# A list of its own in DRAM for the halves of x, a first gather from it, and the last routing ahead of the last two chunks' masks

## The reference

```
qkv = xn @ w_attn.T                      # heads of 16 numbers, 16 heads
phi(x) = elu(x) + 1
per chunk of 128 tokens:
    scores = phi(q) phi(k)^T, masked to the causal half
    num = scores v + phi(q) S ;  den = scores.sum + phi(q) z ;  S += phi(k)^T v ;  z += phi(k).sum
y = (num / den) @ w_proj.T
top  = argmax(xn @ gate_w.T + gate_b + expert_bias)
ffn  = relu(xn @ w1[top] + b1[top]) @ w2[top] + b2[top]
out  = x + y + ffn
```

## Time and profile before

| what | value |
|---|---|
| median of the runs | 510.94 us (509.48 to 511.06) |
| the profiled execution's own time | 512.02 us |
| its span, first to last instruction | 510.2 us |
| what lies around the span | 1.8 us |
| PE, DVE, ACT, POOL busy | 95, 76, 55, 60 % of the span |
| first `g1` of slot 0 | 287.25 us |

### The profile page before, as it was taken

How to read it: one execution, slowest core, us unless ns; L and a number is a source line. 1 busy time by engine, 2 the same in 40 slices (tenths; PEclk the granted TensorE clock), 3 DMA queues, 4 the chain that set the end, 5 groups by cost and what they waited for, 6 DMA issues and landing times.

```text
span 510.2 us, 17893 instructions
## 1 busy us (share of the span) xinstructions
PE 486.4 (95%) x6293; PEld 403.4 (79%) x6293; DVE 389.6 (76%) x849; ACT 280.7 (55%) x540; POOL 307.3 (60%) x497
## 2 busy tenths in 40 slices
PE   7699999999999999999998699999999999999996
PEld 6578887788878888788877678888888888888884
DVE  3678898988989888898789177766776776776774
ACT  3447887888887878877885033333333333333330
POOL 5666888889898798878763523344344344344222
PEclk9989999999999999999999899999999999999999
DMA  8614575665665665655443512132212212210000
GB/s 260 221 44 120 182 212 168 194 190 180 201 176 169 191 195 186 200 168 183 135 148 106 188 35 75 53 90 68 66 56 65 84 53 79 74 50 28 22 17 2
DMA packets 34306, 62.91 MB, mean 123 GB/s; under 512 B 5677, under 2 KB 10030, under 8 KB 34096
## 3 DMA queue, kind: packets, MB, share of 16 engines
q1 hardware_dynamic: 29232, 49.17, 30.9%
q0 software_dynamic: 4992, 12.60, 8.2%
HBM read 51.00 MB, written 13.50 MB: 126 GB/s over the span
## 4 chain that ended last, share of the span: by engine, by line
PE 88%; DVE 3%; issue 3%; POOL 2%; ACT 2%; DMA 1%; DVEq 0%; POOLq 0%; ACTq 0%
PE ps L654 21%; PE ps L667 20%; PE ps L401 8%; PE ps L516 6%; PE ps L443 6%; PE ps L472 6%; PE ps L456 5%; PE ps L419 4%; PE ps L486 4%; PE ps L502 3%; PE ps L623 2%; PE ps L426 1%; PE ps L508 1%; PE ps L384 1%; DMA AR<-scr,AR 1%
## 5 line engine op out<-in xcount | busy, mean ns | idle before, releaser
L654 PEld LDWEIGHTS ps<-AR,W 128*128 x1872 | 131.5, 99 | 40.2 <-issue 1.2
L654 PE MATMUL ps<-AR,W 128*128 128x128 f16 x1872 | 155.9, 220 | 0.9 <-ACT AR L1216 0.9
L667 PE MATMUL ps<-W,ST 128*128 x624 | 150.5, 326 | 0.7 <-DVE ST L1057 0.7
L1225 ACT ACTIVATE ST<-ST 128x512 f16<-128x512 f32 x78 | 49.2, 630 | 104.6 <-DVE ST L1045 103.0
L1386 POOL DMA_INDIRECT out<-AR x39 | 39.8, 1021 | 106.4 <-DVE AR L1077 105.2
L1045 DVE SCALAR_TENSOR_TENSOR ST<-ps,TAs,B1S 128x512 f32<-128x512 f32 x78 | 58.4, 749 | 52.1 <-PE ps L654 49.6
L753 DVE TENSOR_TENSOR AR<-ps,CT 128x512 f32<-128x512 f32 x128 | 82.0, 684 | 3.2 <-PE ps L443 3.2
L1321 POOL TENSOR_TENSOR W<-ST,W 128x512 f16<-128x512 f32 x64 | 74.8, 1169 | 12.5 <-ACT W L1159 6.3
L1381 POOL DMA_INDIRECT AR<-scr,AR x39 | 50.1, 1285 | 31.4 <-issue 12.8
L1057 DVE SCALAR_TENSOR_TENSOR ST<-ST 128x512 f16<-128x512 f32 x78 | 53.6, 687 | 15.6 <-ACT ST L1225 15.6
L401 PE MATMUL ps<-xT,WA 128*128 128x128 f16 x768 | 48.9, 221 | 3.4 <-ACT xT L1109 3.4
(11 more groups left out here) (147 smaller groups left out, 787.0 us busy)
## 6 DMA issues: line engine op xcount, KB each, us to landing
ST<-in_w SPq DMA_DIRECT2D x128, 256.0 KB, 4.2
scr<-XR SPq DMA_DIRECT2D x32, 256.0 KB, 2.1
XR<-in_x SPq DMA_DIRECT2D x32, 128.0 KB, 4.6
AR<-in_b SPq DMA_DIRECT2D x1, 1024.0 KB, 5.3
AR<-in_wall SPq DMA_DIRECT2D x2, 388.0 KB, 4.1
AR<-scr,AR POOLq DMA_INDIRECT x39, 3.6
out<-AR POOLq DMA_INDIRECT x39
ST<-in_cst SPq DMA_DIRECT2D x1, 576.0 KB, 4.8
```

The costliest lines, as they stand in the source:

```text
L654: a = e.matmul(dst, W[:, off:off + 57472][:, bass.ds(place_of(s), 128)], XT16[s % 2][:, xl * 256 + k * 128:xl * 256 + (k + 1) * 128], star ...
L667: a = e.matmul(PS[4 + s % 2][:, 0:w], src[h % 4][:, fs], W[:, off:off + 57344 + w][:, bass.ds(place_of(s), w)], start=(f == 0 and w == 512 ...
L1225: e.activation(HH[h % 4], H32[h % 2], ACT.Relu).then_inc(a_hh, 1)
```

## The change: what it does

The two halves of x get a DRAM list of their own, `scr16`, which SP fills chunk by chunk once they are made (32 more stores of 128 KB). The first NX0 = 3 slots take the halves from it, by gathers of their own (`gather_x16`) into `X0`, so that they need no result of the attention; the whole rows are still gathered from `scr` for every slot, into NG = 8 buffers now (they are the `XR` buffers), for `rest` in slots 0 to 2 and for everything from slot 3 on. DVE routes group 3 in the last turn and right behind it, ahead of the masks of chunks 30 and 31. PE moves `place(3)` and the 32 matmuls for `ids` up, and the last two steps of chunk 31's attention (`yt2`, `pr`) between the pieces of slot 0. ACT and POOL take the last eight quarters behind the loop, in a new order. `rest(s)` moves one slot later.

```diff
+        NG, NX0 = 8, 3
+        XG = [XR[(5 + i) % 8][:, :] for i in range(NG)]
+        X0 = [XR[4][:, 0:256].bitcast(F16)] + [WAF[:, 512 * i:512 * i + 512] for i in range(NX0 - 1)]
 # SP
+            def store_x16(c):
+                e.wait_ge(S["xl"], c + 1)
+                e.dma_start(scr16[c * 128:(c + 1) * 128, :], X16[c % R]).then_inc(d_s16[c % R], 16)
...
+            store_res(NC - 3)
+
+            e.wait_ge(S["pv"], NC)
             e.dma_start(B2, b2).then_inc(d_b2, 16)
+            store_res(NC - 2)
+            store_res(NC - 1)
 # PE, behind the loop
+            place(3)
+            inter(NC - 2)
+            warm(70)
+            (the 32 matmuls for ids)
             yt1(NC - 3)
-            inter(NC - 2)
-            yt2(NC - 3)
             pv(NC - 2)
             scores(NC - 1)
+            yt2(NC - 3)
             pr(NC - 3)
...
             yt1(NC - 1)
-            warm(24)
-            yt2(NC - 1)
-            pr(NC - 1)
 # PE, second phase
+                if s < NX0:
+                    e.wait_ge(d_g16[s], 16)
+                    x16 = X0[s]
...
+                if t == 3:
+                    yt2(NC - 1)
+                if t == 5:
+                    pr(NC - 1)
 # DVE, second phase
+                if s == 0:
+                    res(NC - 1)
...
-                    rest(s)
+                if 1 <= s <= NS:
+                    rest(s - 1)
 # ACT, behind the loop
+            split(NW - 8, 1)
+            vh(NC - 1)
+            y1(NC - 3)
+            split(NW - 7, 4)
+            y1(NC - 2)
+            y2(NC - 3)
+            split(NW - 3, 3)
+            y1(NC - 1)
+            y2(NC - 2)
 # POOL, behind the loop
-            e.wait_ge(a_xg0, 4)
+            e.wait_ge(v_ox, 4)
+            w_lo(NW - 8)
+            km(NC - 1)
+            for n in range(NW - 7, NW - 1):
+                w_lo(n)
...
+            e.wait_ge(v_ids, 1)
+            gather_x16(0)
+            w_lo(NW - 1)
+            for s in range(1, NX0):
+                gather_x16(s)
+            for c in range(NC - R, NC):
+                e.wait_ge(d_scr[c % R], 16 * (c // R + 1))
             for s in range(NG):
+                if s == NG - 1:
+                    e.wait_ge(t_tx, 1)
                 gather(s)
```

More of the change, by code:

```diff
@@ L211, in program @@
         pk = ar(6656 + 2 * NS, NP, I32)
-        XT16 = [ar(6144 + i * 256, 256, F16) for i in range(2)]
+        XT16 = [ar(i * 256, 256, F16) for i in range(2)]
         H32 = [ST[:, i * 512:(i + 1) * 512] for i in range(2)]
@@ L269, in program @@
         d_scr = [sem(f"d_scr{i}") for i in range(R)]
+        d_s16 = [sem(f"d_s16{i}") for i in range(R)]
         d_wall = [sem(f"d_wall{k}") for k in range(2)]
@@ L275, in program @@
         d_gat = [sem(f"d_gat{i}") for i in range(NG)]
+        d_g16 = [sem(f"d_g16{i}") for i in range(NX0)]
         d_sca = [sem(f"d_sca{i}") for i in range(3)]
@@ L590, in tensor @@
             st(NC - 2)
+            place(3)
+            inter(NC - 2)
+            warm(70)
+            for c in range(NC):
+                if c % 16 == 0:
+                    e.wait_ge(v_eq, c // 16 + 1)
+                if c % 8 == 0:
+                    e.wait_ge(v_ao, c // 8 + 1)
+                a = e.matmul(PS[1][:, 0:NS], AO[c // 8][:, :, c % 8], EQS[:, :, c], start=(c == 0), stop=(c == NC - 1))
+            a.then_inc(t_ids, 1)
             yt1(NC - 3)
-            inter(NC - 2)
-            yt2(NC - 3)
             pv(NC - 2)
             scores(NC - 1)
+            yt2(NC - 3)
             pr(NC - 3)
+            yt1(NC - 2)
             e.wait_ge(S["t32"], n_state(NC - 2))
-            warm(30)
-            yt1(NC - 2)
-            place(3)
             inter(NC - 1)
@@ L605, in tensor @@
             yt1(NC - 1)
[L606 to L621 removed]
+            def tx(s):
+                if s < NX0:
+                    e.wait_ge(d_g16[s], 16)
+                    x16 = X0[s]
+                else:
+                    e.wait_ge(d_gat[s % NG], 16 * (s // NG + 1))
+                    x16 = XG[s % NG][:, 0:256].bitcast(F16)
                 for i in range(4):
@@ L976, in vector @@
                     places(0)
-                    places(1)
+                    pick_a(3)
+                    pick_b()
+                    pick_c(3)
+                    ahead(3)
                 if on(p - 4):
@@ L985, in vector @@
             phi(NC - 1)
[L986 to L1001, removed]
             bases()
@@ L1029, in vector @@
             scales_ffn()
+            y(NC - 1)
+            res(NC - 2)
             at = {}
@@ L1207, in scalar, with split @@
                     exp(p - 1)
-                for n in q[2:] if p < NC + 2 else ():
-                    w_scale(n)
-                    w_hi(n)
+            def split(first, n):
+                for i in range(first, first + n):
+                    w_scale(i)
+                    w_hi(i)
+            split(NW - 8, 1)
[7 more added lines that the diff above has]
+            y2(NC - 2)
             def tx(s):
@@ L1323, in gpsimd @@
             nn_begin(1)
-            for p in range(NC + 5):
+            for p in range(NC + 1):
                 if p == 0:
```

106 lines of the change are left out of this document (63 added, 43 removed).

## The result

The changed kernel takes 518.51 us (median of 4 runs, 517.27 to 519.75) against 510.50 us (4 runs) of the kernel before: a ratio of 1.016, 95% interval 1.013 to 1.019. It is slower by 8 us.

What follows compares the result with a forecast made beforehand. PE was taken to bound the kernel, with the change of phase behind the loop deciding. 0.25 + 3.9 + 0.8 = +5.0 us on 512.02 gave 517.0, or 515.9 us in median terms, range 510.0 to 519.0.

Steps and rivals of the forecast that it cites:

- Extra stores: In the loop: 32 stores of 128 KB through SP were taken to cost nothing, at most 3 us.
- Start of the tail: Last turn: eight small DVE operations replace places(1) ahead of res(28), moving res(28) and phi(31) by +1.4 us.
- Contention: DVE's routing beside four w_lo on POOL: meetings over two-input operations, to_slots and places included, cost 2.6 us.
- the sign that was named: Expected in the changed profile: L904, L908 or places (L967) longer than 0.7 us beside a w_lo.
- Both chains to T0': Drain to first g1: POOL's gather chain and PE's chain with its register load end +0.25 us later than before.
- T0': Start of the first g1 in the changed kernel, forecast at 287.5 us against 287.25 before.
- From T0' to the fourth `tx`: From first g1 to tx(3): res(31), store, POOL's wake, gathers and landing take 15.9 us against 12.0, +3.9 us.
- The clock behind that wait: Behind PE's wait ahead of the fourth tx: a granted clock of 0.50 may follow, taken as 0.8 us.
- No contention: Rival, chance 0.18: everything behind the last places comes 2.6 us earlier, T0' = 285.0, time 512.6 to 513.4 us.
- Later still: Rival, chance 0.10: contention of 4.6 us and half clock at T0' and behind tx(3), +8.6, 519.5 us.
- The faster one: Rival, chance 0.12: PE doesn't wait for DVE in the tail, T0' = 280.0, tx(3) 3.3 us earlier, about 507.6 us.

Runs made afterwards that it cites:

- e4_list: The kernel before plus the 32 stores and slots 0 to 2 gathered from the list, old order otherwise: 509.2 us, ratio 0.999 to the kernel before.
- e1_four: The changed kernel with four slots instead of three taken from the list of halves: 515.0 us, ratio 1.009 to the kernel before.
- f1_gate: The changed kernel with POOL's w_lo(57) held until the last places is made: 517.4 us, ratio 1.014 to the kernel before.
- f2_warm: The changed kernel with 112 instead of 70 warm matmuls ahead of the 32 for ids: 520.9 us, ratio 1.021 to the kernel before.
- f4_all: The changed kernel with four list slots, res(29) earlier, w_lo(57) held for places, second-bias load held for the first gather: 509.4 us, ratio 0.999.
- f3_b2: The changed kernel with res(29) moved up and the 1 MB second-bias load held until the first gather of halves landed: 517.8 us, ratio 1.016.
- e2_order: The changed kernel with slot 3's whole rows gathered first, ahead of slots 0 to 2: 513.1 us, ratio 1.005 to the kernel before.
- h1_order: g1_warms with slot 4's whole rows gathered second instead of fifth: 507.0 us, ratio 0.995 to the kernel before.
- g1_warms: f4_all with 54 warm matmuls put where PE waits in the drain: 508.5 us, ratio 0.997 to the kernel before.

## Why the prediction was right, and where it was not

Slower, forecast 515.9 us with 510.0 to 519.0; measured 518.5. Sign and range held; the forecast rise of 5.0 us was 8.0 by the medians and 6.5 by the profiled pair. By its steps:

- **Extra stores, nothing.** Right (e4_list; `phi` at 236.41 against 236.31).
- **Start of the tail, +1.4 us** on `phi(31)`. Right: +1.41.
- **Contention, 2.6 us.** The mechanism was right and the place wrong. It measured 3.31 us and fell on `bases` and `own_slot`; `to_slots` and `places` ran at 0.48 and 0.69 us, since POOL was done at 267.6, so the sign that was named (L904, L908 or L967 above 0.7 us) did not come. The last `places` ended at 272.3, not 271.3. A second meeting was not in the sum at all: the small operations for the packed experts met the last three `w_lo` (L1054 0.88 us, L1058 0.90, L1061 1.89, against 0.19, 0.17 and 0.17 before), the first of them ahead of `res(29)`. The rule of the Trainium skill that was weighed there, "GPSIMD Engine Reference", key points, on instructions with two SBUF inputs, agrees with L917 (1.07 us) against L925 (0.22, one input from PSUM); on `to_slots` and `places` no run here shows it, since they never ran beside a `w_lo`.
- **Both chains to T0', +0.25 us.** It measured +1.46. `y2(29)`, behind which both chains stand, ended at 278.56 instead of 277.1, and the delay went through: `pr(30)` ended at 286.26 instead of 284.7, the load behind it at 287.4 instead of 286.3, `tx(0)` and the copy took 1.26. The lines show where the 1.46 us at `y2(29)` come from. In the changed kernel, the last masks of chunk 30, the second half of `pv(30)`, `scores(31)` and `yt2(29)`:

```profile
273.99 1.28 DVE L785 TENSOR_TENSOR AR<-ps,CT 128x512 f32<-128x512 f32 x2
275.41 1.08 PE L495 MATMUL ps<-AR 128*32 128x128 f32 x16 [0.31 <-DVE AR L785]
276.43 1.35 PE L466 MATMUL ps<-AR 32*128 32x256 f32 x16
277.71 0.44 PE L531 MATMUL ps<-CT,AR 128*128 128x128 f32 x2
```

In the kernel before, the same masks, the same two groups of matmuls and what followed them:

```profile
262.88 1.28 DVE L753 TENSOR_TENSOR AR<-ps,CT 128x512 f32<-128x512 f32 x2
264.30 0.65 PE L472 MATMUL ps<-AR 128*32 128x128 f32 x16 [0.27 <-DVE AR L753]
264.88 1.15 PE L443 MATMUL ps<-AR 32*128 32x256 f32 x16
265.95 1.13 PE L516 MATMUL ps<-AR 128*128 128x256 f32 x4
```

The masks of chunk 30 were done at 275.27, not 274.7: 0.57 us, mostly from the contention (3.31 against 2.6). From there the two groups took 2.44 us, where before, at full clock, they took 1.79: 0.65 us is half clock, and 0.24 us is the rest of `pv(30)`, which was priced at 0.4. So two terms of this step were mis-sized: every matmul of the drain was priced at full clock, and the small operations beside POOL at nothing but the 2.6 us. Until 277.3 DVE works without a gap and PE waits for it, so half clock that ends there costs little, 0.65 us. Where it lasts until PE is what the drain waits for (269 to 287 us, as in e1_four, f1_gate, f2_warm and f4_all's profile) it costs more: some 3 us by f4_all's two groups, and f2_warm, with 13 us of it instead of 7, was 2.4 us slower than the changed kernel. A second condition was left out of the chain: the register load also waits for the packed experts, ready at 285.02 with the end of L1061. It began at 285.3, right behind the start of `pr(30)` at 285.13, so in the changed kernel the two came within 0.2 us of each other, and f3_b2, with an earlier drain, ran into the other one.
- **From T0' to the fourth `tx`, 15.9 us.** 15.48, by the steps named: `res(31)` at T0' + 4.7 (5.2 forecast), a store of 2.0, 0.9 until POOL's first gather at 296.27, steps of 1.30, 1.71 and 1.31, landing 3.6 behind the fourth. Forecast +3.9, measured +3.50. The forecast's 4.4 for `res(31)` at full clock does not follow from its own terms, which give 3.9 (2.0 + 0.4 + 1.1 + 0.42); it took 5.2 between that and 5.9. e1_four and e2_order show that the wait costs what it seems to.
- **The clock behind that wait, +0.8 us.** +1.66: half clock from 304.2 to 307.5, the upper side of what was given; 4.14 us of idle time, not the 2.4 to 3 forecast, stood ahead of it, because PE came to the fourth `tx` 11.3 us behind T0' and not 13.5: the clock was at 1.00 from T0' on, and the wait of 0.68 us for `low` that stood at 295.13 before is gone.
- **The sum.** The forecast is 2.6 us under the median. The steps make +1.2 (T0'), -0.4 (to the fourth `tx`) and +0.9 (the clock behind it), some 1.6 us in all. The other 1.0 us is no cost of the kernel: 1.1 us were taken off because the profiled execution before lay above its median, but that of the changed kernel (518.55) lies on its own.
- **Rivals.** "No contention" is answered by f1_gate: with 3.3 us of it taken away the first `g1` came 0.2 us earlier, since the clock stayed low until PE was what the drain waits for. "Later still" came near in its time, by half clock behind the fourth `tx` alone; its 8.6 us count the 0.8 of the forecast beside its own 0.7 + 0.9. The faster one decides from T0' below 281.8. No kernel reached that; h1_order gains by another route, with 283.59 and no wait at `tx(3)`. The routing ahead does pay once the drain's clock, the load beside the gather, POOL's contention and the wait for whole rows are dealt with: 24.5 us from `scores(30)` to `g1` instead of 27.9.

That the parts add up to more than their sum (4.7 us alone, 8.9 together) is measured; I have no experiment for each pair, so how much of it is the clock's group and how much waits that hid one another stays open.

## What to carry to other kernels

When a step is taken out of a wait, follow the same buffer to its next reader: here the first gather was freed from the attention, and the fourth paid for it, behind three more gathers on one queue. Order a queue by when each row is wanted, not by its number. Warm matmuls that fill waits are part of the schedule: whoever takes them out or shifts them has to price the code behind them at both clocks, and check the spread of the runs against the mean clock before one profile is believed.

## What the runs showed of the hardware

- The granted clock fell to 0.50 at 274 us in f2_warm, where PE had waited 0.56 us once since 262, and at 270 in f1_gate, where it had waited 0.16. "TensorE: Matmul & The Clock Gate" of the Trainium skill, What's actually happening, has the level follow how busy PE has been; that more filled waits kept it at 1.00 in g1_warms agrees, but the busy share that the profile shows does not tell the two apart (11.43 of 12 us in f2_warm), and a search for long idle gaps would not have found this fall.
- A gather of 128 rows of 1 KB took 6.2 us with a 1 MB load issued 0.4 us behind it, and 3.7 when the load waited.
- DVE operations of a single small input wait for POOL too: a cast of eight words (L1061 of the changed kernel) took 1.89 us, a TENSOR_SCALAR of eight words 1.16 (L915 in f2_warm), against 0.17. L1061 ended at 285.02, the `w_lo` beside it at 284.99. A TENSOR_REDUCE of 64 words (L930, at 265.42, in the midst of the four `w_lo`) kept its 0.22 us.
